# Moving the local work of the last two blocks into group 0, and reordering weight loads, in a four-part layer on one core

## The reference, cut to what matters

```
x = x + pooled(x)     # scores = v . tanh(x W1 + b1); per token a softmax over a masked set of tokens
                      # (prefix, suffix, or all others), weighted mean of x, divided by the count
x = x + stencil(x)    # zX * (left - 2x + right) along channels + zY * (before - 2x + after) along tokens
                      # + zR * x * (1 - x), reflecting at the edges
x = x + adapter(x)    # y = x + relu(x Wd + bd) Wu + bu, then LayerNorm with ln_g, ln_b
x = x + block(x)      # ctx = running sum of x with decay; gate wg = sigmoid([x, ctx] Wg + bg)
                      # mod = 0.5 + sigmoid(gelu(x Wn1 + bn1) Wn2 + bn2), two running sums of x*wg*mod
                      # soma = gelu(x Wsoma + b) times sigmoid(blended sums Wtemp + b), through Wout, LayerNorm
```

## Time and profile before

| | |
|---|---|
| median of 3 runs | 736.37 us (736.3 to 740.94) |
| the profiled execution | 737.53 us |
| its span, first to last instruction | 735.7 us |
| PE busy | 673.4 us (92%), weight loads 493.6 us |
| DVE busy | 541.0 us (74%) |
| ACT busy | 353.5 us (48%) |
| POOL busy | 178.3 us (24%) |
| mean granted TensorE clock | 0.965 of full speed |
| moved by DMA | 87.87 MB, 119 GB/s over the span |

### The profile page before, as it was taken

The page is one execution under the profiler, slowest core; times in us unless marked ns, Lnnn a source line. Parts: engine busy times, 40 slices in busy tenths (PEclk is TensorE's granted clock), DMA queues, the critical chain, the costliest instruction groups (busy, mean ns, idle before and its releaser), DMA issues.

```text
span 735.7 us, 7942 instructions
## 1 busy us (share of the span) xinstructions
PE 673.4 (92%) x2808; PEld 493.6 (67%) x2808; DVE 541.0 (74%) x737; ACT 353.5 (48%) x710; POOL 178.3 (24%) x220
## 2 busy tenths in 40 slices
PE   4969979165899999999999999999999999999996
PEld 1545444133677877878687868787877788687874
DVE  2665888776898588759766986697578758775964
ACT  0143377445355634653474357344724553465144
POOL 5002456665152300320132022102310310021001
PEclk9989999677899999999999999999999999999999
DMA  7896899679930970294049306721780050013001
GB/s 214 288 352 199 162 235 310 199 133 334 327 64 0 172 115 0 76 188 80 1 105 181 58 1 142 160 42 52 136 157 1 0 115 2 0 27 89 0 2 57
DMA packets 52470, 87.87 MB, mean 119 GB/s; under 512 B 8256, under 2 KB 10304, under 8 KB 52430
## 3 DMA queue, kind: packets, MB, share of 16 engines
q0 software_dynamic: 16896, 33.56, 27.8%
q1 hardware_dynamic: 32046, 53.79, 20.7%
q10 hardware_dynamic: 3488, 0.01, 0.3%
HBM read 64.27 MB, written 23.09 MB: 119 GB/s over the span
## 4 chain that ended last, share of the span: by engine, by line
PE 77%; DVE 7%; DMA 6%; POOL 3%; ACT 3%; issue 2%; SPq 1%; POOLq 0%; ACTq 0%; DVEq 0%
PE bank L1054 20%; PE bank L1056 20%; PE bank L1055 20%; PE bank L1094 3%; PE bank L1110 3%; PE bank L955 3%; PE bank L1157 2%; PE bank L1119 2%; DMA xr<-beside_scratch 2%; PE bank L1084 2%; DMA local_scratch<-xts 2%; DMA beside_scratch<-xb 2%; PE bank L1050 1%; DMA xts<-in_xT 1%; POOL xts L545 1%
## 5 line engine op out<-in xcount | busy, mean ns | idle before, releaser
L592 POOL TENSOR_TENSOR rs_a<-ss_a,consts 128x1 f32<-128x1 f32 x32 | 12.9, 404 | 196.9 <-ACT hb L743 196.1
L1513 DVE TENSOR_TENSOR_SCAN tr<-alpha,carry,tr 128x512 f32<-128x512 f32 x48 | 58.9, 1271 | 0.0
L1507 DVE SCALAR_TENSOR_TENSOR tr<-wgb,blend_w,mod 128x512 f32<-128x512 f32 x64 | 46.0, 750 | 10.7 <-ACT mod L768 9.8
L1054 PE MATMUL bank<-xh,wg_l 128*128 128x512 f32 x128 | 52.8, 413 | 0.0
L1054 PE MATMUL bank<-th,wg_l 128*128 128x512 f32 x128 | 52.0, 406 | 0.0
L1056 PE MATMUL bank<-xh,wg_h 128*128 128x512 f32 x128 | 50.1, 391 | 0.0
L1055 PE MATMUL bank<-xl,wg_h 128*128 128x512 f32 x128 | 50.1, 391 | 0.0
L1056 PE MATMUL bank<-th,wg_h 128*128 128x512 f32 x128 | 50.1, 391 | 0.0
L1055 PE MATMUL bank<-tl,wg_h 128*128 128x512 f32 x128 | 49.9, 390 | 0.0
L545 POOL TENSOR_TENSOR xts<-xb 128x2040 f32<-128x2040 f32 x8 | 29.7, 3713 | 64.1 <-DVE xb L1402 53.0
L783 ACT ACTIVATE carry<-tr 128x2 f32<-128x2 f32 x32 | 6.5, 203 | 72.6 <-DVE tr L1513 72.6
(11 more groups left out here) (247 smaller groups left out, 1987.1 us busy)
## 6 DMA issues: line engine op xcount, KB each, us to landing
x2b<-beside_scratch POOLq DMA_DIRECT2D x12, 1024.0 KB, 9.3
xr<-rows_scratch POOLq DMA_DIRECT2D x10, 1024.0 KB, 10.3
xb<-in_x SPq DMA_DIRECT2D x8, 1024.0 KB, 14.5
beside_scratch<-xb SPq DMA_DIRECT2D x8, 1024.0 KB, 9.8
result<-xr SPq DMA_DIRECT2D x7, 1024.0 KB, 4.4
local_scratch<-xts SPq DMA_DIRECT2D x6, 1024.0 KB, 11.4
x2b<-local_scratch SPq DMA_DIRECT2D x6, 1024.0 KB, 5.5
x2b<-rows_scratch POOLq DMA_DIRECT2D x6, 1024.0 KB, 15.0
```

The costliest lines, as they stand in the source:

```text
L1054: pe.matmul(acc, wl, xh_, start=start, stop=False)
L1507: ve.scalar_tensor_tensor(t[:, d], w, blend_w[:, d, k:k + 1], mod[:, d], ALU.mult, ALU.mult).then_inc(tr_in, 1)
L1513: ve.tensor_tensor_scan(t[:, d], alpha[:, 1 + d:2 + d].broadcast_to([P, GN]), t[:, d], 0.0 if first else carry[:, k, 1 + d:2 + d], ALU.mul ...
```

## The change

The work is the same, instruction for instruction. What moves:

1. mix_local(6), mix_local(7), scale_beside(5) to (7), by_local(6), (7) and stencil(6), (7) stand inside group 0's lists on ScalarE and VectorE; the copies wn2_rep go ahead of by_local(5).
2. The sums of batch 1 (`normalise(1)`, `sums_low(1)`) and the transposes, down and up of unit 0 stand earlier; on GpSimd the rstd steps of unit 0 stand ahead of add_before(1) and channels(4), and channels(4) waits in addition until ln_apply of unit 0 is done (`x3_done`).
3. SP loads wg in halves behind store_beside(2) and store_beside(3); wtemp now comes before wout, and wout waits for the last two local stores.
4. In SBUF the pair th, tl changes places with wout's tiles; the waits of trace_hi and trace_lo of group 0 on local stores fall away, and one stands before wout's high half.

```diff
             wgb = sb2("wgb", [P, 2, GN])
+            th = sb2("th", [P, KE, GN], F32R)
+            tl = sb2("tl", [P, KE, GN], F32R)
             wo_h = sb2("wo_h", [P, KE, E], F32R)
             wo_st, wo_l = staged("wo_l", [P, KE, E], s2)
-            th = sb2("th", [P, KE, GN], F32R)
-            tl = sb2("tl", [P, KE, GN], F32R)
...
                     store_beside(1)
+                    store_beside(2)
                     sp.wait_ge(hid_mm, 2 * NG)
                     sp.dma_start(wg_st[:, 0:KE], chunks(wg)[:, 0:KE]).then_inc(w_in[0], 16)
-                    store_beside(2)
                     store_local(2)
+                    store_beside(3)
                     sp.dma_start(wg_st[:, KE:], chunks(wg)[:, KE:]).then_inc(w_in[1], 16)
-                    store_beside(3)
+                    store_local(3)
                     load_x2(2)
-                    store_local(3)
...
-                    sp.wait_ge(pool_mm, B * NT)
-                    sp.dma_start(wo_st[:], chunks(wout)).then_inc(w2_in[2], 16)
                     store_beside(7)
                     store_local(7)
                     beside_landed(sp, 1, 2)
                     beside_landed(sp, 1, 3)
                     sp.dma_start(wt_st[:], chunks(wtemp)).then_inc(w2_in[1], 16)
+                    sp.wait_ge(local_out[GROUPS - 2], 16)
+                    sp.wait_ge(local_out[GROUPS - 1], 16)
+                    sp.dma_start(wo_st[:], chunks(wout)).then_inc(w2_in[2], 16)
...
                     add_before(0)
-                    add_up_bias(1)
                     add_after(0)
                     channels(2)
+                    add_up_bias(1)
                     weight_low(0, wn1_h[:], wn1_l[:], wn1_st[:])
-                    add_before(1)
                     channels(3)
-                    add_after(1)
-                    weight_low(1, wg_h[:, 0:KE], wg_l[:, 0:KE], wg_st[:, 0:KE])
-                    channels(4)
                     for c in range(GT):
                         rstd(ln_ss, ss_a, EPSILON, rs_a, c, ln_p, ln_rs, c)
+                    add_before(1)
+                    po.wait_ge(x3_done, GT)
+                    channels(4)
+                    weight_low(1, wg_h[:, 0:KE], wg_l[:, 0:KE], wg_st[:, 0:KE])
+                    add_after(1)
                     weight_low(2, wg_h[:, KE:], wg_l[:, KE:], wg_st[:, KE:])
                     channels(5)
...
                             add_before(g + 2)
                             if g == 0:
-                                weight2_low(2, wo_h[:], wo_l[:], wo_st[:])
+                                weight2_low(2, wt_h[:], wt_l[:], wt_st[:])
                             add_after(g + 2)
-                        if g == 0:
-                            weight2_low(3, wt_h[:], wt_l[:], wt_st[:])
                         if g < LAST:
                             for c in range(GT):
                                 rstd(ln_ss, ss_a, EPSILON, rs_a, GT * (g + 1) + c, ln_p, ln_rs, c)
+                            if g == 0:
+                                weight2_low(3, wo_h[:], wo_l[:], wo_st[:])
...
-                    scale_beside(5)
-                    mix_local(6)
-                    scale_beside(6)
-                    mix_local(7)
-                    weight_hi(0, ws_h[:], ws_st[:])
-                    scale_beside(7)
+                    scale_beside(4)
+                    mix_local(5)
                     for g in range(GROUPS):
                         adapted = g < LAST
                         n1_gelu(g)
+                        if g == 0:
+                            mix_local(6)
+                            scale_beside(5)
...
                         keep_traces(g, 1)
                         if g == 0:
-                            weight_hi(2, wo_h[:], wo_st[:])
+                            weight_hi(0, ws_h[:], ws_st[:])
+                            scale_beside(7)
...
                         keep_traces(g, 3)
+                        if g == 0:
+                            act.wait_ge(local_out[GROUPS - 2], 16)
+                            weight_hi(2, wo_h[:], wo_st[:])
                         trace_hi(g, 3)
...
                     pooled(1, 0)
+                    x2_transposes(0)
                     pooled(1, 1)
-                    x2_transposes(0)
                     pooled(1, 2)
+                    down(0)
                     pooled(1, 3)
-                    down(0)
-                    pooled(1, 4)
-                    pooled(1, 5)
                     up(0)
-                    for c in range(6, 10):
+                    for c in range(4, 11):
                         pooled(1, c)
```

More of the change, by code:

```diff
@@ L613, in _ @@
                     add_shift(0)
+                    channels(6)
                     add_up_bias(2)
-                    channels(6)
                     channels(7)
@@ L864, in _ @@
                     sums_hi(1)
-                    mix_local(2)
                     for j in range(NG):
@@ L869, in _ @@
                         probT_evict(1, j)
+                    mix_local(2)
                     wg_hi(2, wn1_h[:], wn1_st[:])
+                    act.wait_ge(params_set, S_PARAMS)
+                    x2_evict(0)
                     scale_beside(2)
                     mix_local(3)
-                    act.wait_ge(params_set, S_PARAMS)
-                    x2_evict(0)
-                    scale_beside(3)
-                    wg_hi(0, wg_h[:, 0:KE], wg_st[:, 0:KE])
                     act.wait_ge(cols_in, 16 * 3 * B)
@@ L901, in _ @@
                         mod_sigmoid(g)
+                        if g == 0:
+                            scale_beside(6)
+                            mix_local(7)
                         keep_traces(g, 0)
@@ L1584, in _ @@
                     normalise_out(1)
+                    normalise(1)
                     x1(0, 12)
[L1586 removed]
+                    sums_low(1)
                     x1(0, 13)
[L1588 removed]
                     x1(0, 14)
                     x1(0, 15)
+                    x1(1, 0)
+                    by_local(2)
                     stencil(2)
[L1592 to L1594 removed]
+                    for c in range(1, 4):
+                        x1(1, c)
+                    for c in range(GT):
+                        y_sum(0, c)
+                    x1(1, 4)
+                    x1(1, 5)
                     by_local(3)
                     stencil(3)
[L1597 to L1599 removed]
                     for c in range(GT):
[L1601 to L1602 removed]
+                        ln_weigh(0, c)
                     x1(1, 6)
                     for c in range(GT):
[L1605 to L1607 removed]
                         ln_apply(0, c)
+                    for c in range(7, 11):
+                        x1(1, c)
                     by_local(4)
                     stencil(4)
[L1611 to L1613 removed]
                     x1(1, 11)
+                    x1(1, 12)
                     x3_lo(0)
[L1616 to L1625 removed]
+                    for c in range(13, NT):
+                        x1(1, c)
                     for d in range(2):
@@ L1628, in _ @@
                     assert n["p"] == S_PARAMS, n["p"]
+                    by_local(5)
+                    stencil(5)
                     for g in range(GROUPS):
@@ L1631, in _ @@
                         logits(g, 0)
+                        if g == 0:
+                            by_local(6)
                         traces(g, 0)
+                        if g == 0:
+                            stencil(6)
                         logits(g, 1)
+                        if g == 0:
+                            by_local(7)
                         blend_traces(g, 0)
@@ L1636, in _ @@
                         trace_lo(g, 0)
+                        if g == 0:
+                            stencil(7)
                         logits(g, 2)
```

45 lines of the change are left out of this document (9 added, 36 removed).

## The result

| | kernel before | changed kernel |
|---|---|---|
| median | 736.88 us (6 runs, 736.30 to 740.94) | 744.75 us (6 runs, 741.32 to 745.17) |
| profiled execution (span) | 737.53 us (735.7) | 744.61 us (742.8) |
| ratio | | 1.0102, 95% interval 1.008 to 1.0124 |

The change makes the kernel 1.0% slower (7.9 us between the medians, 7.1 us between the spans). 741 us was forecast, within 1% of no change; the ratio lies just past that 1%.

A forecast was written before the change was run, and what follows sets the result against it. TensorE was taken to bound seven of eight groups, leaving 32 us of earlier waits to win. Terms -1.7, -12.8, +7.5, +2.4, +9.0 made +4.4 us on the 736.4 us median: 741 us, range 726 to 749.

The forecast's parts named there:

- the turns on the port pair: VectorE and GpSimd lock a shared SBUF port pair per instruction; the waiting one gets in between two instructions of the other.
- the chain through wtemp: Block 7's scaling, its store, the wtemp load, then ScalarE's high half, behind which VectorE's work waits; fourth trace_lo 1.6 us later.
- Stage A: Up to the last ln_apply of unit 0: ends at 135.7 instead of 137.9 us, 2.2 us earlier.
- Stage B: From there to the start of group 0: alternating VectorE and GpSimd work of 26.3 us, start at 162.0, gain 1.7 us.
- Stage C: Group 0's start to soma_in: wn2's wait goes, wsoma's low half is late; soma_in at 201.1 us, TensorE waits 7.5 us.
- Stage D: Up to the fourth trace_lo: wtemp load of 8.2 us lands at 211.7, trace_lo ends at 227.0, 1.6 us later than before.
- 743.7 us: End time expected if the wtemp load took 11.0 us, with all queues interleaving on the same 16 DMA engines.
- a wait in temporal ended by trace_lo: Expected sign in the trace: TensorE stands in temporal until VectorE's trace_lo is done.
- Stage E: Up to the output product: wout's low half meets ln_apply and product, adding 3.5 us; product_lo at 245.1, output 4.4 us later.
- The sum: All terms over the whole kernel: -1.7, -12.8, +7.5, +2.4 and +9.0 give +4.4 us.
- wn2's wait, -12.8: TensorE in group 0: the 10.9 us wait for wn2's copies and its slow clock go, 12.8 us gained.
- The swap of addresses: The th, tl pair against wout in SBUF, with the local-store waits it removes: costs nothing and gives nothing.

The follow-up runs named there:

- fourth run: The kernel before, with only VectorE's two copies of wn2 moved up behind x1(1,15): 734.50 us, ratio 0.9966.
- 8: The kernel before, with wn2's copies behind x1(1,15) and n1_gelu(0) behind scale_beside(6) on ScalarE: 733.79 us, ratio 0.9966.
- ninth: The kernel before, with wn2's copies and n1_gelu(0) early and soma_in waiting for one low half instead of two: 730.84 us, ratio 0.9922.
- 10: The ninth run's kernel, with GpSimd's low half of wout moved behind the rstd steps: 730.77 us, ratio 0.9922.
- first run: The changed kernel, with ScalarE's high half of wtemp behind relu(1) instead of in front of keep_traces(0,2): 739.39 us, ratio 1.0022.
- second: The changed kernel, with GpSimd issuing the accumulating transfer of group 2 behind the low half of wtemp: 738.88 us, ratio 1.0026.
- third run: The changed kernel without GpSimd's low half of wout; the output product reads the high half twice: 742.18 us, ratio 1.0062.
- fifth run: The changed kernel, with scale_beside(7) in front of wsoma's high half on ScalarE: 737.38 us, ratio 1.0009.
- sixth run: The changed kernel, with SP asking for wout only when wtemp has landed: 744.51 us, ratio 1.0105.
- seventh run: The changed kernel, with GpSimd's channels(5) also waiting for VectorE's four x3_lo of unit 0: 743.00 us, ratio 1.0082.
- twelfth run: The changed kernel without GpSimd's wait for x3_done in front of channels(4): 746.61 us, ratio 1.0125.

## Why the prediction was right, and where it wasn't

The forecast was 741 us and the measured 744.75; the turns on the port pair and the chain through wtemp came as forecast. The term that was off is the wtemp load, 8.2 us in the sum and 12.7 measured.

**What bounds.** Right: nothing changes behind 340 us, and all of the loss arises between the start of group 0 and its output product.

**Stage A.** Forecast: the last ln_apply ends at 135.7, 2.2 us earlier; it does at 136.5. Of the 1.4 us gained, 1.15 are there already behind x1(0,11), which ends at 94.1 in place of 95.3, ahead of everything that the change moves on VectorE: that is how much executions differ. The kernels with the order of before (before, runs 4, 8, 9, 10) take 42.6 to 43.2 us from there to the last ln_apply, those with the new order (changed, runs 1, 2, 3, 5, 6) 42.2 to 42.9. The earlier place gave about 0.5 us, near the forecast's lower end.

**Stage B, the turns on the port pair.** Forecast: 26.3 us from the last ln_apply to group 0, so 162.0; measured 25.1, and 161.64. The 0.8 us that stage A lacked and the 1.2 us that this stage had too much nearly cancel, which is luck. The forecast gain of 1.7 us looks like 2.1 in the two profiled executions, but counted from x1(0,11) the same two sets of kernels take 68.3 to 69.0 and 67.3 to 68.0 us, about 1 us. The alternation is shown by the x3_lo row (8.90 us with a low half and channels(5) in it) and by the seventh run, which takes one of the two out and gets 3.4 us back.

**Stage C, the low half of wsoma.** Forecast: soma_in at 201.1 behind 7.5 us; measured 201.06 behind 9.37. One link was another than I had it: by_local(7) is held by mix_local(7), 3.48 us, which waits for the store of block 5 (13.1 us from issue to landing), and not by channels(7). The two links are about as long, so the time came out right by luck. And TensorE was there at 191.7, not at 193.6, so that its wait is longer by the same 1.9 us and the sum is not touched.

**Stage D, the mis-sized term.** The mechanism is right and shown by three runs: ScalarE stands for the wtemp load in front of VectorE's work. The size isn't. "I take 8.2, nearly the middle: 211.7" between 5.6 and 11.0; the load took 12.7 and landed at 214.98, past my upper end. That is 4.5 us more than the term; 1.2 us of it came back because the load was issued at 202.25 and not at 203.5. It is the accumulate, which is issued 1.3 us ahead of the load: 12.7 and 12.5 us with it ahead (change, sixth run), 8.0 without, 7.0 where the load goes first. Of the rows that I weighed the 11.0 was the right neighbour, since the accumulate's packets ran beside that load. The 5.6 us store, issued at 107.67, had an accumulate issued 0.6 us ahead of it as well (at 107.05), but the first packets of that one came only at 112.0, when the store was nearly through. So the order of issue alone doesn't say who is slowed; what counted in each of these traces is whose packets came first. The Trainium skill ("DMA: Bandwidth & Descriptors", section "Issuing engines are not separate DMA queues"), by which I gave 743.7 us, came nearest to the 744.75. The same page's section "Queues, rings and completion order" has each engine take packets from its queues in turn. The trace agrees from 210 to 212 us (128 and 129 packets) and shows what a count of packets leaves out: by my estimate from these counts and the shares of time an accumulate's packet took 0.17 us and one of SP's 0.10, so the load got less than half of the time. And two transfers of 1 MB beside the load are not alike: wout behind it on the same queue costs it nothing, an accumulate of GpSimd ahead of it nearly 5 us.

**Where TensorE waits for stage D.** I wrote "a wait in temporal ended by trace_lo". There was none. The wait is one step earlier, at up(1), for relu(1), which stands behind the same high half on ScalarE. The fourth trace_lo ended at 229.65 instead of 227.0, 2.6 us late out of the 3.3 by which the load landed late, since the steps behind it took 14.7 us and not 15.3. I had followed VectorE's instructions behind the blocked one and not ScalarE's own.

**Stage E.** Forecast: product_lo at 245.1, 18.1 us behind the fourth trace_lo; measured 247.57, 17.9 us behind it, so late by what stage D was late. The meeting costs VectorE the 3.3 us that remain over the 14.6 of before, as forecast, but the end only 1.4 to 2.6 us (third run): without it TensorE itself is at the output at 244.26. The waits of 0.2 us that the view shows in the output understate it: the first four pieces of output take 1.1 us longer than in the third run.

**The sum.** +4.4 us were forecast, the spans differ by 7.1: 2.7 us more, and the fourth trace_lo is 2.6 us later than forecast, which is the load's miss. The medians differ by 0.8 us more than the spans, since the profiled execution of before was 0.65 us over its median.

**wn2's wait, -12.8.** From the start of group 0 TensorE came to soma_in 14.3 us earlier than before, 1.5 more than the term. It could, because the change also moves n1_gelu(0) and the wait for w2_lo. Alone, in the kernel before, it is 2.2 us (fourth run), and 5.9 only with the other two gates (ninth). The change made all three moves and then lost what they give through the wtemp chain.

**The swap of addresses.** "Cost nothing and give nothing" is half right. It couldn't be undone alone: with the old addresses trace_lo(0,0) waits for a store of block 7, which needs stencil(7), and that stands behind it on VectorE. It is what the new order needs. What it gives by itself wasn't tried.

**Left open.** Why a packet of the accumulate holds an engine longer than one of a plain load, and why its first packets come 3.4 us behind the issue here and 5.0 us at 107.05 in the kernel before; no run took it apart further. The earlier sums of batch 1, the earlier transposes, down and up of unit 0, and the halves of wg on SP weren't tried alone.

## What to carry to other kernels

A wait that is removed uncovers the one that ended just before it, so list for the waiting instruction every semaphore that it and its producers wait for, on each engine, before the wait's length is put down as gain: 10.9 us here were 2.2, and 5.9 when all three gates went. A load on which an engine's queue stands should have its packets through before those of an accumulating transfer come (5.9 and 7.4 us in the second and fifth runs), and the instruction that waits for it belongs behind whatever doesn't need it (5.4 us in the first run); the two weren't tried together. If two costs were measured in rows that differ in what ran beside them, look at the packets of each queue while the transfer was under way, and take the row with the same neighbour and not the middle.

## What the runs showed of the hardware

- With an accumulating 1 MB transfer of GpSimd issued 1.3 us ahead of it a plain 1 MB load of SP took 12.5 to 12.7 us; with one issued 1.8 us behind it 7.0 us, and the accumulate 14.4; without one 8.0. A plain 1 MB load behind on the same queue changed nothing (12.7 and 12.5).
- While both queues had packets (210 to 212 us) each moved 64 a microsecond, at 70% of the engines' time for the accumulate and 40% for SP's queue (the shares overlap a little). The accumulate's first packets came 3.4 us (changed kernel), 4.4 us (fifth run) and 5.0 us (before, issued at 107.05) behind its issue.
- The turns on the shared port pair between VectorE and GpSimd: one GpSimd operation gets in between two neighbours of a row of four short operations of VectorE. The row of x3_lo took 2.5 us alone, 5.5 with one large GpSimd operation in its way (seventh run) and 8.9 with two (changed kernel); the row of ln_apply 2.7 alone and 10.6 with two (twelfth run).
- After waits of 9.2, 9.4 and 7.1 us TensorE's granted clock was 0.50. The eight matmuls of up(1) took 6.1 us behind such a wait, and 3.6 us in the kernel before, without one and at a granted clock of 1.00.
